# Four layers on one core: the first layer's weight loads ahead of the couples', and the third layer's weights from split operands

## The reference

```python
# layer 0: one expert for each block, the largest of its 8 numbers
expert = jnp.argmax(cond, axis=-1)
up   = jnp.einsum('bsd,bhd->bsh', x, W_up[expert]) + b_up[expert][:, None, :]
gate = jnp.einsum('bsd,bhd->bsh', x, W_gate[expert]) + b_gate[expert][:, None, :]
x = x + jnp.einsum('bsh,bdh->bsd', jax.nn.silu(up) * gate, W_down[expert]) + b_down[expert][:, None, :]
# layer 1: a base matrix plus LoRA, weighed by cond
x = x + (jnp.einsum('btc,oc->bto', x, W_base) + b_base
         + 2.0 * jnp.einsum('bter,eor,be->bto', jnp.einsum('btc,erc->bter', x, As), Bs, cond))
# layer 2: a masked mix of 8 matrices, weighed by cond
w_bot = jnp.einsum('bg,got->bot', cond, weight * mask[None, :, :])
x = x + jnp.einsum('bnt,bot->bno', x, w_bot) + bias
# layer 3: the best 2 of 8 experts for each block, and a shared one (GELU MLPs of width 512)
x = x + sum of the two, by their weights + shared(x)
```

## Time and profile before

| | |
|---|---|
| three runs, median (lowest to highest) | 158.79 us (157.98 to 159.51) |
| the profiled execution, its own time | 159.42 us |
| its span, first to last instruction | 157.4 us |
| PE busy | 149.7 us (95%) |
| DVE, POOL, ACT busy | 113.0, 93.5, 71.5 us |
| granted TensorE clock, mean | 1.000 |
| HBM read | 24.71 MB |

### The profile page before, as it was taken

How to read it: one execution, slowest core, us unless ns; L and a number is a source line. 1 busy time by engine, 2 the same in 40 slices (tenths; PEclk the granted TensorE clock), 3 DMA queues, 4 the chain that set the end, 5 groups by cost and what they waited for, 6 DMA issues and landing times.

```text
span 157.4 us, 3159 instructions
## 1 busy us (share of the span) xinstructions
PE 149.7 (95%) x1078; PEld 135.8 (86%) x1078; DVE 113.0 (72%) x229; ACT 71.5 (45%) x138; POOL 93.5 (59%) x95
## 2 busy tenths in 40 slices
PE   6999994899999999999999999999999999999992
PEld 2369994799998689999999989999989899999881
DVE  3785662466798767768786887696778977768772
ACT  2765441346055455444543635435454443346550
POOL 1002999999502400958995775998593989990000
PEclk9999999999999999999999999999999999999999
DMA  3999999996000568377076749158619119000051
GB/s 72 406 324 313 332 414 401 401 389 225 18 0 0 159 177 236 101 222 245 4 242 249 249 117 305 45 158 300 212 22 332 53 42 348 16 0 0 0 201 69
DMA packets 13336, 29.11 MB, mean 185 GB/s; under 512 B 1272, under 2 KB 7944, under 8 KB 13192
## 3 DMA queue, kind: packets, MB, share of 16 engines
q1 hardware_dynamic: 12896, 27.71, 51.9%
q10 hardware_dynamic: 424, 1.20, 1.9%
HBM read 24.71 MB, written 1.05 MB: 164 GB/s over the span
## 4 chain that ended last, share of the span: by engine, by line
PE 71%; SPq 8%; DMA 7%; DVE 7%; issue 3%; ACT 2%; ACTq 0%; DVEq 0%
PE pair L530 22%; PE acc L579 10%; PE pair L537 9%; PE pair L520 8%; DMA ring<-experts 6%; PE acc L564 5%; PE acc L588 5%; PE pair L467 4%; SPq L256 3%; SPq L259 3%; PE acc L429 2%; PE pair L499 2%; PE acc L475 2%; DVE hid L752 2%; ACT hid_hi L422 2%
## 5 line engine op out<-in xcount | busy, mean ns | idle before, releaser
L743 DVE TENSOR_TENSOR hid_lo<-hid,hid_hi 128x512 fp32r<-128x512 f32 (+1 forms) x41 | 40.1, 981 | 18.5 <-ACT hid_hi L422 17.9
L363 POOL TENSOR_TENSOR duo_lo<-raw_duo,duo_hi 128x512 fp32r<-128x512 f32 x36 | 46.3, 1286 | 2.9
L422 ACT ACTIVATE hid_hi<-hid 128x512 fp32r<-128x512 f32 (+1 forms) x41 | 25.4, 622 | 48.1 <-DVE hid L752 47.1
L360 POOL CAST duo_hi<-raw_duo 128x512 fp32r<-128x512 f32 x36 | 30.4, 845 | 22.1 <-PE acc L579 22.1
L530 PE MATMUL pair<-x_duo,duo_hi 128*128 128x256 f32 x192 | 35.9, 284 | 0.1
L752 DVE TENSOR_TENSOR hid<-pair,act 128x512 f32<-128x512 f32 (+1 forms) x49 | 32.8, 672 | 3.8 <-PE pair L530 2.8
L403 ACT ACTIVATE act<-pair 128x512 f32<-128x512 f32 x48 | 28.2, 587 | 7.3 <-PE pair L530 5.5
L530 PEld LDWEIGHTS pair<-x_duo,duo_hi 128*128 128x128 f32 x192 | 29.9, 189 | 1.0 <-DVE hid L752 0.3
L530 PE MATMUL pair<-x_duo,duo_lo 128*128 128x256 f32 x96 | 27.1, 283 | 0.0
L520 PE MATMUL pair<-x_hl,shared_hi 128*128 128x512 f32 x64 | 20.3, 399 | 0.0
L467 PE MATMUL pair<-x,ring 128*128 128x128 f32 x128 | 17.2, 277 | 2.8 <-DMA ring<-experts 2.8
(11 more groups left out here) (94 smaller groups left out, 209.0 us busy)
## 6 DMA issues: line engine op xcount, KB each, us to landing
raw_duo<-experts SPq DMA_DIRECT2D x12, 768.0 KB, 5.0
ring<-experts SPq DMA_DIRECT2D x16, 386.5 KB, 5.9
raw_solo<-experts SPq DMA_DIRECT2D x8, 768.0 KB, 5.0
x_duo<-x_hl SPq DMA_DIRECT2D x24, 128.0 KB, 3.6
x<-xT ACTq DMA_DIRECT2D x1, 1024.0 KB, 6.0
raw_solo<-shared SPq DMA_DIRECT2D x1, 768.0 KB, 6.9
out<-lora_raw SPq DMA_DIRECT2D x3, 256.0 KB, 2.8
w_sb<-w SPq DMA_DIRECT2D x1, 512.0 KB, 4.0
```

What stands on the lines that cost most here:

```text
L360: pool.tensor_copy(duo_hi[:, j % HALVES, piece(n)], raw_duo[:, j % RAWS, piece(n)])\
L363: pool.tensor_tensor(duo_lo[:, j % HALVES, piece(n)], raw_duo[:, j % RAWS, piece(n)], duo_hi[:, j % HALVES, piece(n)].bitcast(F32), ALU.su ...
L422: act.activation(hid_hi[:, k % SPLITS, at], hid3[:, u % PAIRS, at], ACT.Copy)\
L743: dve.tensor_tensor(hid_lo[:, k % SPLITS, at], hid3[:, u % PAIRS, at], hid_hi[:, k % SPLITS, at].bitcast(F32), ALU.subtract).then_inc(hid_ ...
```

## The change

SP reads expert numbers into registers in two goes (four, then twelve) instead of one before each load, and issues ring loads 8 to 11 right behind the shared weights, ahead of the wait for `slots_done` and of the first couple; their waits for `x1_done` stay. Then follow couple 0, ring 12 and 13, couple 1, ring 14 and 15.

The eight products of w2 and `y_delta` become three float32r passes each. ScalarE casts w2 to its high part in two halves of 128 x 512 before its first copy, GpSimd computes the low part in two halves, and VectorE the high and low part of `y_delta` (128 x 256) right behind it, each operation waiting for the one before. The two parts of w2 use the tiles that later hold the shared weights' parts. PE waits for all three of VectorE's operations, and at products 0 and 4 for GpSimd's halves.

```diff
+        w2_hi, w2_lo = (t[:, 0:E * P].rearrange("p (e n) -> p e n", e=E) for t in (shared_hi, shared_lo))
...
             def load0(b):
-                at = sp.value_load(at_row[0:1, b:b + 1], min_val=0, max_val=E - 1)
+                at = expert0[b]
...
             sp.wait_ge(at_done, 1)
-            for b in range(SLOTS0):
+            expert0 = list(values(mybir.EngineType.SP, at_row[0:1, 0:4], E))
+            for b in range(4):
+                load0(b)
+            expert0 += values(mybir.EngineType.SP, at_row[0:1, 4:B], E)
+            for b in range(4, SLOTS0):
                 load0(b)
             sp.dma_start(shared_sb, shared).then_inc(shared_in, 16)
+            for b in range(SLOTS0, SLOTS0 + 4):
+                load0(b)
             sp.wait_ge(slots_done, 1)
             duo_expert = values(mybir.EngineType.SP, slot_row[0:1, SLOTS:SLOTS + 2 * DUOS], E)
             load_duo(0)
-            load0(SLOTS0)
-            load0(SLOTS0 + 1)
+            for b in range(SLOTS0 + 4, SLOTS0 + 6):
+                load0(b)
             load_duo(1)
-            for b in range(SLOTS0 + 2, B):
+            for b in range(SLOTS0 + 6, B):
                 load0(b)
...
# gpsimd, first of all
+            for k in range(0, E, E // 2):
+                at = slice(k, k + E // 2)
+                pool.wait_ge(w2_hi_done, 1 + 2 * k // E)
+                pool.tensor_tensor(w2_lo[:, at, :], w2_sb[:, at, :], w2_hi[:, at, :].bitcast(F32), ALU.subtract)\
+                    .then_inc(w2_lo_done, 1)
...
# scalar, ahead of the copies of L387
+            act.wait_ge(w2_in, 16)
+            for k in range(0, E, E // 2):
+                at = slice(k, k + E // 2)
+                act.activation(w2_hi[:, at, :], w2_sb[:, at, :], ACT.Copy).then_inc(w2_hi_done, 1)
...
# tensor
-            pe.wait_ge(ydelta_done, 1)
-            pe.wait_ge(w2_in, 16)
+            pe.wait_ge(ydelta_done, 3)
...
-                ins = pe.matmul(prep[n % 2][:, (k % 2) * B * R:(k % 2 + 1) * B * R], w2_sb[:, k, :],
-                                y_delta[:, :, :].rearrange("p b j -> p (b j)"), start=True, stop=True)
+                if k % (E // 2) == 0:
+                    pe.wait_ge(w2_lo_done, 1 + 2 * k // E)
+                for m, (w, y) in enumerate(((w2_hi, y_hi), (w2_hi, y_lo), (w2_lo, y_hi))):
+                    ins = pe.matmul(prep[n % 2][:, (k % 2) * B * R:(k % 2 + 1) * B * R], w[:, k, :],
+                                    y[:, :, :].rearrange("p b j -> p (b j)"), start=(m == 0), stop=(m == 2))
...
# vector, behind y_delta
+            dve.wait_ge(ydelta_done, 1)
+            dve.tensor_copy(y_hi[:, :, :], y_delta[:, :, :]).then_inc(ydelta_done, 1)
+            dve.wait_ge(ydelta_done, 2)
+            dve.tensor_tensor(y_lo[:, :, :], y_delta[:, :, :], y_hi[:, :, :].bitcast(F32), ALU.subtract)\
+               .then_inc(ydelta_done, 1)
```

More of the change, by code:

```diff
@@ L180, in build_kernel @@
         y_delta = sb("y_delta", [P, B, R])
+        y_hi = sb("y_hi", [P, B, R], F32R)
+        y_lo = sb("y_lo", [P, B, R], F32R)
         lora_raw = sb("lora_raw", [P, B, P])
@@ L215, in build_kernel @@
         ydelta_done, bsw_done = sem("ydelta_done"), sem("bsw_done")
+        w2_hi_done, w2_lo_done = sem("w2_hi_done"), sem("w2_lo_done")
         prep_mm, prep_copied = sem("prep_mm"), sem("prep_copied")
```

## The result

The changed kernel takes **159.93 us** in the median of 20 runs (158.66 to 160.9), the kernel before 158.55 beside it (157.42 to 160.1). The ratio is **1.0082**, 95% interval 1.0052 to 1.0112: a small loss, clear of zero, and smaller than the 1% that I had said a measurement of this kernel can tell. It missed the sign and, by 0.03 us, the range. A second series of the same kernel gave 1.0118 (1.0048 to 1.0189).

The account below looks back on a forecast made before the run. PE was taken as the bound, with time to gain from its waits or less PE work. -3.16 + 2.7 + 0.3 = -0.2 us took the profiled 159.42 to 159.2, given as 158.6 after 0.63 for the median; range 156.0 to 159.9.

Parts of the forecast that it names:

- PE waits at blocks 8 and 10, 3.16 us, and they go away: Layer 0: issuing ring loads 8 to 11 ahead of the couples removes both PE waits, -3.16 us.
- VectorE takes turns with GpSimd, slot product +2.7 us: Start, split weights: VectorE waits through both GpSimd subtractions, slot product at 16.5 instead of 13.74, +2.7 us; forecast case, chance 0.62.
- No block here: Rival at the start: GpSimd does not hold VectorE up, only 0.3 us is lost there, total 156.2 us; chance 0.20.
- What is late next: loads 12 to 15, +0.3 us, bounds 0 to 1.6: End of layer 0: SP's waits for loads 8 to 11 delay the couples, leaving blocks 14 and 15 no margin, +0.3 us.
- the couples' loads turn into the wait: Rival in layer 0: couples held behind load 11, DMA runs empty, ring 14 lands late, total 159.9 us; chance 0.13.
- two signs that I had named for a wrong forecast: Chain behind y_lo starting before 9.5 us, or block 14 waiting for the ring by more than 1 us.
- The last block within half a microsecond of its old place: Expected sign in the profile after: layer 0's last block stays within half a microsecond, though both ring waits are gone.
- the three terms: The forecast's sum: ring waits gone -3.16, VectorE's turns with GpSimd +2.7, late loads 12 to 15 +0.3 us.
- The early fill buys little, DMA is the limit: Rival in layer 0: some 2 us of the ring's wait stay, total 160.4 us; chance 0.05.
- Everything behind layer 0 shifts one for one: Later layers take their pace from PE, so a shift of block 15 passes to the end one for one.

Follow-up runs that it names:

- new order: Kernel before with only SP's changed load order and reads in two goes, layer 2's weights as before: 159.82 us, ratio 1.0035; repeated, ratio 1.0001.
- The control: The kernel before, run and profiled once more unchanged: ratio 1.0036, profiled execution 158.04 us.
- couples last: Changed kernel with the slots' wait, the 24 reads and both couples' loads moved behind ring 15: 160.04 us, ratio 1.008.
- interleaved: Kernel before with reads in two goes, couple 0 after ring 8 and couple 1 after ring 12: 157.39 us, ratio 0.9952.

## Why the prediction was wrong, point by point

*PE waits at blocks 8 and 10, 3.16 us, and they go away* — right in the trace: neither block waits in any kernel with the new order. But 3.16 was one execution's figure. The control, same kernel, has 2.2 us (blocks 8 to 10). The profiled execution of before was 0.87 us above the median of twenty, and I priced the gain from it. In the end I took 0.63 us off for that slow execution as well; if it was slow by its long waits, as the control suggests, the same microseconds were counted twice.

*VectorE takes turns with GpSimd, slot product +2.7 us* — the mechanism was right and confirmed by taking GpSimd's halves away, and the rival *No block here* is out. The size was 2.08. I charged both halves in full, 2.56; y_hi and y_lo lost 1.91, because bs_w and y_delta, queued back to back, were not interrupted and GpSimd waited for them first. In these traces the turn passed at y_hi and y_lo, each of which waits for a semaphore, and not between VectorE's back-to-back operations; I had not reckoned with that, and no run tests that the gap is the reason. The rule of the Trainium skill ("SBUF — State Buffer", "Who interferes with whom") is borne out where the rows of before had nothing: y_hi's copy, one input from SBUF, is blocked too, 1.25 us against 0.29.

*What is late next: loads 12 to 15, +0.3 us, bounds 0 to 1.6* — **this is the step that failed.** It measured 1.8 us in one profile and 2.5 in the other, beyond the upper bound. I had seen that SP holds the couples behind its waits, and let the stream behind them start with the landing of a lone 768 KB load, 4.5 us, from the earlier trace rows. (Even that load was not quite alone: the second solo was on its way beside it until 38.4 us.) But the first couple now comes behind rings 9 to 11 and has 12 and 13 beside it: it took 6.1 us (30.4) in the first profile and 6.7 in the second. The issue was forecast well: measured from block 1, it is 0.1 us off. From the first couple's landing on, everything comes late by nearly the same amount, 1.6 to 1.9 us in the first profile, ring 14 with it, so the extra 1.6 us at the head of the stream are the error there. The trace of before had the nearer number, 6.6 us for the same load under traffic. I took the lone load of the same size instead of the same load in its traffic.

That price is not all of it. In the second profile of the new order the first couple did land after 4.5 us, and PE still waited 1.3 us at block 14, because ring 12 and 13 landed 1.6 and 3.0 us behind the couple where I had put 1.0 and 2.0. So the spacing of 1.0 us a ring load, taken from a full stream, was too short as well; why it is longer here stays open.

The rival "the couples' loads turn into the wait" got 0.13; it is what happened: its threshold was 7.3 us for load 14, which took 8.9 and 9.0. Its words on DMA were too strong: DMA did not run empty, it was 43 to 86% busy. Of the two signs that I had named for a wrong forecast, this one came, block 14 later than 1 us (1.26); the other did not. "The last block within half a microsecond of its old place" came true (36.58 to 36.92), but by luck: the early expert row hid half of what the three terms left over.

With the measured sizes the same sum comes out: -3.16 + 2.08 + 1.79 = +0.71, the difference of the two traces. The ratio says 1.3 us, the medians differ by 1.4. The rest fits the smaller waits of a typical execution of before (2.2) and the longer ones after (2.5); in half-pace starts the split costs little but the waits stay. That is an account in sizes, from two profiles of each kernel, and no profile of before in a half-pace start was caught, so the last 0.6 us or so are argued and not shown.

*"The early fill buys little, DMA is the limit"* (0.05) — wrong in its reason, though 1.8 us of waiting did stay: with the couples last or interleaved, the waits of blocks 12 to 15 vanish or fall to 0.8 us with the same bytes to move.

*Everything behind layer 0 shifts one for one* — right: 118.4 to 119.0 us in all profiles but one. That one (couples last) shows the condition, that GpSimd's splits end before VectorE's low parts of x begin.

## What to carry to other kernels

A load put ahead of a queue's wait moves every load behind that wait: price the last of them, under the traffic it will meet, not the first. The wait found in one profile is not yet the kernel's wait: two profiles of the unchanged kernel had 3.2 and 2.2 us, so take a second one before pricing a gain of 3 us. And before work goes to an idle GpSimd, look for what VectorE does in the same microseconds: two short operations of 0.7 us became 2.6.

## What the runs showed of the hardware that was not expected

- TensorE can go over to its full pace at 3.9 to 5.5 us or only at 9.0 to 10.6 us in one and the same kernel, so that eight records take 3.86 or 6.05 us, with the clock column at 1.00 in both. The runs don't show what decides: up to 5.46 us the records of the two executions compared above look the same.
- A VectorE copy of float32 to float32r, 128x256 in SBUF, is shut out by a GpSimd subtraction like a two-input operation is (1.25 us against 0.29), while VectorE operations already queued back to back ran at their old length in every profile with the split.
- A couple's load, 768 KB, landed after 4.0 us at the least (late in layer 3) and after up to 9.3 us in the traffic of layer 0. Two executions of one kernel differ by a microsecond in it: the first couple took 5.5 and 4.5 us under the new order.
